# One decoder kernel, mamba stage: the state inputs of two slots are spread back to back, the sums run two slots behind, and the small work has other slots

## What is computed

```
xz = x @ in_w.T;  xi, z = split(xz)                 # 512 features each
u = silu(causal_conv4(xi) + conv_b)
xdbl = u @ xp_w.T                                   # 16 for dt, 16 for B, 16 for C
dt = softplus(xdbl[:, :16] @ dt_w.T + dt_b)
h[t] = exp(dt[t] * A) * h[t-1] + (dt[t] * u[t]) * B[t]     # 512 features x 16 states
y[t] = sum_n(h[t][:, n] * C[t][n]) + u[t] * D
out = (y * silu(z)) @ out_w.T
```

## Time and profile before

| what | value |
|---|---|
| median of three runs | 2918.92 us |
| the profiled execution | 2914.82 us |
| its span | 2913.0 us |
| PE matmul busy, of the span | 94% |
| PE weight load busy | 62% |
| DVE / ACT / POOL busy | 75% / 60% / 53% |
| scans, instructions and mean | 1024, 1203 ns |
| hC, instructions and mean | 512, 2369 ns |
| dA, instructions and mean | 1024, 710 ns |
| spread products, instructions and busy | 8192, 595.9 us |
| sum products, instructions and busy | 4120, 563.5 us |

### The profile page before, as it was taken

How to read it: one execution, slowest core, us unless ns; L and a number is a source line. 1 busy time by engine, 2 the same in 40 slices (tenths; PEclk the granted TensorE clock), 3 DMA queues, 4 the chain that set the end, 5 groups by cost and what they waited for, 6 DMA issues and landing times. The chain is left out here.

```text
span 2913.0 us, 55381 instructions
## 1 busy us (share of the span) xinstructions
PE 2741.4 (94%) x19289; PEld 1815.9 (62%) x19330; DVE 2188.3 (75%) x3270; ACT 1756.4 (60%) x2899; POOL 1550.5 (53%) x850
## 2 busy tenths in 40 slices
PE   5999999999999999999999959999999999999996
PEld 2777777777777777777777634545454545454423
DVE  3988988898889889888988768484847474747463
ACT  5778877877877788678768413444444444444332
POOL 1888889888988888898889721111111111111010
PEclk8999999999999999999999979999999999999978
DMA  3022211212220222112112071505050505050500
GB/s 116 31 76 77 70 53 63 97 33 70 81 83 32 76 77 67 56 62 98 33 66 97 8 161 41 78 18 80 15 88 8 89 6 94 2 94 2 79 2 15
DMA packets 113354, 174.50 MB, mean 60 GB/s; under 512 B 15232, under 2 KB 88064, under 8 KB 113056
## 3 DMA queue, kind: packets, MB, share of 16 engines
q1 hardware_dynamic: 113104, 171.34, 23.0%
HBM read 148.38 MB, written 22.94 MB: 59 GB/s over the span
## 5 line engine op out<-in xcount | busy, mean ns | idle before, releaser
L925 DVE TENSOR_TENSOR_SCAN h<-dA,pair 128x512 f32<-128x512 f32 x1024 | 1177.2, 1203 | 142.1 <-PE pair L448 111.5
L1067 POOL TENSOR_TENSOR hC<-h,C_rep 128x1024 f32<-128x1024 f32 x512 | 1197.9, 2369 | 87.1 <-DVE h L925 83.1
L678 ACT ACTIVATE dA<-delta,cols 128x511 f32<-128x511 f32 x1024 | 664.5, 710 | 98.7 <-DVE h L925 97.7
L448 PEld LDWEIGHTS pair<-diagB,duT 64*128 64x128 f32 x8192 | 498.1, 188 | 239.7 <-issue 194.0
L448 PE MATMUL pair<-diagB,duT 64*128 64x128 f32 x8192 | 595.9, 285 | 20.1 <-issue 10.2
L539 PE MATMUL y_bank<-ident,hC 128*128 128x128 f32 x4120 | 563.5, 280 | 9.4 <-POOL hC L1067 7.8
L539 PEld LDWEIGHTS y_bank<-ident,hC 128*128 128x128 f32 x4120 | 442.0, 141 | 73.9 <-POOL hC L1067 10.4
L1791 DVE CUSTOM_DVE_ANT_0 masked<-pair,mask_bias 128x512 f32<-128x512 f32 x512 | 321.9, 687 | 28.3 <-PE pair L1304 14.5
L1864 POOL TENSOR_SCALAR rstd<-mv 128x4 f32<-128x4 f32 x24 | 11.6, 484 | 563.5 <-DVE mv L1643 563.5
L1536 ACT ACTIVATE pr<-pair 128x1024 f32<-128x1024 f32 x256 | 248.5, 1021 | 94.2 <-PE pair L1304 83.8
L448 PE MATMUL general<-xnT,w_in 128*128 128x512 f32 x512 | 253.0, 605 | 5.9 <-ACT zs L678 3.1
(11 more groups left out here) (173 smaller groups left out, 3156.9 us busy)
## 6 DMA issues: line engine op xcount, KB each, us to landing
C_rep<-c_rows SPq DMA_DIRECT2D x128, 512.0 KB, 3.9
w_in<-w_in SPq DMA_DIRECT2D x16, 1024.0 KB, 4.8
qk_parts<-qk_part SPq DMA_DIRECT2D x48, 256.0 KB, 2.5
k_st<-qk_parts SPq DMA_DIRECT2D x48, 256.0 KB, 9.0
q_st<-qk_parts SPq DMA_DIRECT2D x48, 256.0 KB, 8.8
x_in<-x SPq DMA_DIRECT2D x18, 512.0 KB, 4.3
w_out<-w_out SPq DMA_DIRECT2D x17, 512.0 KB, 4.4
mid<-x_out SPq DMA_DIRECT2D x9, 512.0 KB, 6.4
```

The source lines that it names most:

```text
L448: return pe.matmul(o, lhsT, rhs, start=start, stop=stop)
L678: return act.activation(o, i, fn, **kw)
L925: last = dve.tensor_tensor_scan(h[:, g % 4, i, :], dA[:, g % 4, i, :], dBu[:, i, :], 0.0, ALU.mult, ALU.add)
L1067: pool.tensor_tensor(hC[:, g % RING], h[:, g % 4], C_rep[:, 2 * j:2 * j + 2, :], ALU.mult).then_inc(s_hC.sem, 1)
```

## The change

It spreads slots p + 1 and p + 2 one after the other at every even slot, where it spread p + 1 at every slot; SUM_LAG goes from 3 to 2; nearly all tables change; the load of w_in waits for z as well as for xi; and `apart` may leave a place in the rotation of banks empty so that a yb does not follow an xd in its bank. Arithmetic and number of instructions on PE, DVE, ACT and POOL in a unit stay as they are.

```
--- before.py
+++ after.py
@@ -87,41 +87,54 @@
     return before, loop, [key for key in loop if key[0] not in skip]
 
 
-XI_AT = {1: (1, 1), 2: (5, 5), 3: (15, 16), 0: (25, 25)}
-Z_AT = {3: (13, 14), 0: (26, 26), 1: (29, 29), 2: (30, 31)}
-DT_AT = {1: 1, 2: 4, 3: 17, 0: 24}
-TR_AT = {1: 5, 2: 11, 3: 19, 0: 27}
-OP_AT = ((7, 8), (10, 10))
+XI_AT = {1: (0, 0), 2: (8, 8), 3: (10, 12), 0: (26, 26)}
+Z_AT = {3: (14, 14), 0: (25, 25), 1: (28, 29), 2: (31, 31)}
+DT_AT = {1: 2, 2: 5, 3: 17, 0: 23}
+TR_AT = {1: 5, 2: 12, 3: 21, 0: 29}
+OP_AT = ((4, 7), (8, 8))
 XP_AT = (21, 21, 21, 21)
-BT_AT = 23
-NF_AT = (20, 23)
-SUM_LAG = 3
+BT_AT = 24
+NF_AT = (19, 23)
+SUM_LAG = 2
 RING = 4
-BACK_AT = {3: 4, 0: 13, 1: 19, 2: 30}
-
-XI_OUT = {1: 0, 2: 5, 3: 17, 0: 26}
-Z_OUT = {3: 16, 0: 28, 1: 30, 2: 31}
-SUM_OUT = {3: 0, 0: 9, 1: 18, 2: 27}
-SOFT_AT = {1: 0, 2: 4, 3: 18, 0: 25}
-TR_OUT = {1: 4, 2: 13, 3: 21, 0: 29}
+BACK_AT = {3: 2, 0: 10, 1: 18, 2: 28}
+
+XI_OUT = {1: 0, 2: 9, 3: 14, 0: 27}
+Z_OUT = {3: 16, 0: 27, 1: 30, 2: 31}
+SUM_OUT = {3: 0, 0: 9, 1: 17, 2: 25}
+SOFT_AT = {1: 1, 2: 7, 3: 18, 0: 24}
+TR_OUT = {1: 6, 2: 12, 3: 20, 0: 30}
 SILU_AT = 19
 XD_OUT, BT_OUT = 21, 24
-NF_OUT = (20, 24)
-RES_AT = 11
-DIAG_ACT = {1: 28, 3: 30, 5: 30, 7: 31}
-SKIP_AT = {3: 1, 0: 10, 1: 16, 2: 28}
+NF_OUT = (21, 24)
+RES_AT = 9
+DIAG_ACT = {1: 26, 3: 28, 5: 30, 7: 30}
+SKIP_AT = {3: 0, 0: 8, 1: 17, 2: 25}
 FIRST_AT = (14, 18)
-LN_AT = ((11, 11), (14, 14))
-
-TAP_AT = {1: (3, 3, 4), 2: (8, 9, 10), 3: (17, 17, 18), 0: (27, 27, 28)}
-GATE_AT = {3: 4, 0: 15, 1: 20, 2: 31}
-DELTA_AT = {1: 3, 2: 6, 3: 18, 0: 26}
-ADD_AT = (9, 11)
-STATS_AT = ((0, 0, 0), (13, 13, 13))
-
-DU_AT = {1: 2, 2: 6, 3: 17, 0: 24}
-DIAG_POOL = {0: 23, 2: 28, 4: 31, 6: 31}
-RSTD_AT = (3, 11)
+LN_AT = ((10, 11), (16, 17))
+
+TAP_AT = {1: (2, 4, 4), 2: (10, 10, 10), 3: (15, 16, 17), 0: (28, 28, 29)}
+GATE_AT = {3: 4, 0: 12, 1: 21, 2: 30}
+DELTA_AT = {1: 4, 2: 8, 3: 20, 0: 26}
+ADD_AT = (8, 10)
+STATS_AT = ((0, 0, 0), (12, 14, 15))
+
+DU_AT = {1: 3, 2: 9, 3: 19, 0: 25}
+DIAG_POOL = {0: 26, 2: 29, 4: 31, 6: 31}
+RSTD_AT = (6, 14)
+
+
+def apart(keys, banks=3):
+
+    out = []
+    for key in keys:
+        while key[0] == "yb":
+            held = [old for old in out[len(out) - banks::-banks] if old is not None] if len(out) >= banks else []
+            if not held or held[0][0] != "xd":
+                break
+            out.append(None)
+        out.append(key)
+    return out
 
 
 def mamba_keys():
@@ -154,7 +167,7 @@
             keys += [key for _, key in sorted(at)]
         return keys
 
-    return before, batch(4), batch(2) + [("yb", 2 * KI)] + [("op", TT + jj) for jj in range(TT // 2)]
+    return before, apart(batch(4)), apart(batch(2) + [("yb", 2 * KI)] + [("op", TT + jj) for jj in range(TT // 2)])
 
 
 BEFORE, AFTER = "before", "after"
@@ -171,10 +184,13 @@
             held[k] = key
         final = {}
         for n, key in enumerate(loop):
-            final[n % len(banks)] = key
+            if key is not None:
+                final[n % len(banks)] = key
         for name, keys in (("loop", loop), (AFTER, after)):
             held = {}
             for n, key in enumerate(keys):
+                if key is None:
+                    continue
                 k = n % len(banks)
                 self.where[name, key] = (k, ("this", held[k]) if k in held else ("last", final[k]))
                 held[k] = key
@@ -397,6 +413,8 @@
                     if live(M):
                         sp.wait_ge(*G.full(("xi", KI * d + 2), it))
                         settle(sp)
+                        sp.wait_ge(*G.full(("z", KI * d), it))
+                        settle(sp)
                         load_in(d)
                     if live(N):
                         sp.wait_ge(*G.full(("dt", KI * d + 2), it))
@@ -592,8 +610,9 @@
                 for d in range(2):
                     U, N, M = 2 * b + d, 2 * b + d + 1, 2 * b + d + 2
                     for p in range(UP):
-                        if p + 1 < UP or live(N):
-                            spread_du(U, p + 1)
+                        for g in (p + 1, p + 2):
+                            if p % 2 == 0 and (g < UP or live(N)):
+                                spread_du(U, g)
                         sum_states(U, p - SUM_LAG)
                         for i, k in enumerate((3, 0, 1, 2)):
                             if p == BACK_AT[k]:
```

## The result

The changed kernel takes 2850.84 us (median of 4 runs, 2848.7 to 2855.99) against 2918.21 for the one before, a ratio of 0.9771 with a 95% interval of 0.9754 to 0.9788: 67 us faster. The profiled execution has a span of 2854.1 us; the mamba stage ends at about 1594 us instead of 1657.

The account below looks back on a forecast made before the run. PE was taken as the bound. A unit goes from 100.1 to 95.7 + 0.7 + 1.0 + 0.2 + 0.5 = 98.1 us; 14 units plus 1 at the end gain 29 us, giving 2890 us, range 2870 to 2926.

Parts of the forecast that it names:

- PE is the bound: Mamba stage: PE has 98.6 us of work in a unit of 100.1, so work taken off PE shortens it.
- That rival: DVE is the bound already and nothing comes of the change: 2900 to 2925 us, chance 0.18.
- the change of mode: PE between half-row spreads and full-row work: 0.09 us each, two fewer per two slots, 46 us for 256 pairs.
- the list of a unit: PE's work in one batch and direction of 32 slots: 98.6 us before, 95.7 after.
- Two spreads in a row: PE at even slots: second spread taken at 1.0 us, bounds 0.9 and 1.69; 1.69 everywhere would add 177 us, excluded.
- The idle time: PE per unit after the change: 0.7 us loop head, plus waits of 1.0, 0.2 and 0.5.
- the loop's head: PE idle before the first spread of every second unit, 1.41 us; counted as 0.7 us a unit.
- Its places: PE waits around slots 14 to 18, 1.0 us on average; x_proj 0.2; near misses by POOL and ACT 0.5.
- The dt product of slot 17: PE product taking the bank the slot's last tap frees: 0.3 us too early, inside the wait already counted.
- The sum of slot 15 in direction 0: PE sum needing POOL's hC: following POOL's queue from slot 14, reached with -0.15 us to spare.
- The slower rival: Spread p+2 behind scan p at even slots: the meeting costs more than the modes, 2926 or 2946 us, chance 0.15.
- The last unit: End of the mamba stage, set by DVE: gains about nothing, 1 us from one sum fewer after the last scan.

Follow-up runs that it names:

- e5: Changed kernel with the whole sum p-2 placed between the two spreads of an even slot: 2917.05 us, ratio 0.9983 to the kernel before.
- e10: Changed kernel with each of the twelve convolution taps of a unit on DVE working on 16 columns instead of 509 to 511: 2838.1 us, ratio 0.9726.
- e11: Changed kernel with ACT's second normed block at slot 23 instead of 24 and the first diagonals at 27 instead of 26: 2861.2 us, ratio 0.9799.
- e1: Kernel before with only the two spreads back to back at every even slot, old tables and sums three behind: 3060.05 us, ratio 1.0476.
- e8: Changed kernel with block 3's taps and convolution start one slot earlier, and the second normed block at slot 23: 2852.31 us, ratio 0.9786.
- e2: Changed kernel with one spread per slot again, new tables and lag of two kept: 3015.98 us, ratio 1.0326 to the kernel before.
- e3: Changed kernel with sums three slots behind instead of two (SUM_LAG = 3): 3026.38 us, ratio 1.0382 to the kernel before.
- e4: Changed kernel with the first of the 8 transposes of sum p-2 done between the two spreads: 2909.53 us, ratio 0.9965 to the kernel before.

## Why the prediction was right in kind and wrong in size

- **PE is the bound** (98.6 us of work in a unit of 100.1): right. e5 puts 5.6 us a unit of changes of mode back and 4 of them show. The rule under which DVE came first (the Trainium skill, "Perfetto Trace Analysis", "Identifying the Most-Contended Engine": for TensorE the share of its weight loads, or its FLOP utilization, in place of matmul busy time, and occupancy for the others) would have had the change give about 2919. The measurement decides against it here: PE with its loads busy 76% was the bound, DVE with 88% was not. That rival is dead, and e10 says the same of the changed kernel.
- **The term that was mis-sized is the change of mode**, taken as 0.09 us each and 0.18 per pair of slots, 46 us in all. It is 0.35, 89 us. That step failed: the list of a unit went from 98.6 to 93.0 us and not to 95.7. The error was in reading. I took the distance across the border (last couple to first transpose, 0.20 for 0.11) and did not look at the one after it. And I checked it with two sums of 0.93 and 1.02 us that both stood behind a spread: the 0.06 of the second transpose was in both and cancelled. The 16 products of a spread in 1.09 us against 8 x 0.11 = 0.88 would have shown it; I used that very product for the bound of the second spread.
- **Two spreads in a row**, taken at 1.0 us with bounds 0.9 and 1.69: 0.99. The exclusion of 1.69 was right. That the second spread takes 0.99 where one entered from full-row work takes 1.09 is the same missing 0.10 us, and the sum did not book it: it took 1.0 and left the two slots at 4.06, where 3.88 was measured.
- **The idle time**: 0.7 for the loop's head and 1.7 of waits, 2.4 in all, predicted; 95.8 - 93.0 = 2.8 measured. The total is near, in part by luck. The head is less: the idle time put down to issue before spreads fell from 8.9 to 2.4 us, 0.2 a unit. The waits are more. The rows of loads above give, over 13.9 units, 1.0 us a unit for scans, 0.5 for hC, 0.4 for xnT and 0.35 for the last tap, 2.25 in all; as loads can wait without cost, these shares are rough.
- **Its places** held in part. The dt product of slot 17 waits for the last tap, as said, and duT is close to late (e11). From spread 18 to spread 19 it is 4.52 us in the changed kernel and 3.85 in e10, where the taps are short (means of six units of direction 1). The sum of slot 15 in direction 0, put at -0.15 us, is late for its hC. Not foreseen were z of slot 25 waiting for xnT (0.5 us of idle PE in each unit of direction 0), and that scan 0 too is late at the head of the loop (DVE stands 1.34 us idle before it, put down to issue) and with it spread 2. The head (first two rows) and the sum (third) in one unit of direction 0:

```profile
261.93 1.16 PE L466 MATMUL pair<-diagB,duT 64*128 64x128 f32 x16 [0.30 <-issue]
263.37 1.16 PE L466 MATMUL pair<-diagB,duT 64*128 64x128 f32 x16 [0.28 <-DVE h L944]
...
316.13 1.09 PE L557 MATMUL y_bank<-ident,hC 128*128 128x128 f32 x8 [0.56 <-POOL hC L1086]
```

- **The slower rival** (the meeting costs more than the modes) did not come true with these tables. It is the nearest to what e1 did, but e1 lost 140 us, and its one wait that was tested was two engines crossing within one slot, which totals of a pair do not hold.
- **The last unit** gained nothing, as said: 92.7 us before and 93.4 after.

The account closes: 15 units x 4.2 us (99.6 to 95.4 on average from the first scan of the stage to that of the last unit) is 63 us; the other 4 of the 67 are within the spread of the runs (2849 to 2856 for the changed kernel).

What stays open is what the rest of PE's idle 2.8 us would give back: about 0.2 are the loop's head and 0.6 come from the taps. For the other 2.0 the rows name scans, hC and xnT, but no run separates them, and e8 and e11 show that a wait taken out here can come back elsewhere.

## What to carry to other kernels

Read the price of a border between two kinds of work from the distance of starts over the whole run of each kind, entered and not entered from the other kind, not from the one interval at the border. When a wait is moved ahead of an engine's small work, look up in every other engine's list who uses that work in the same slot: e1 and e2 came out 140 and 96 us slower than the kernel before and e3 176 us slower than the changed kernel, where the whole change gained 67. And a version whose parts are each 3% slower alone can be 2% faster together, so test such parts by putting one cost back into the whole (e4, e5), not only by adding them one at a time.

## What the runs showed of the hardware that was not expected

A change between spreads (two products of 64 rows side by side) and products or transposes of 128 rows costs at two places: 0.09 us before the first product of the new kind, and another 0.10 us (into spreads) or 0.06 us (into transposes) before the second. A pair of changes, into spreads and back, is 0.35 us, seen as 4.23 to 3.88 us for two slots and as 3.79 to 4.14 us when one transpose was put between two spreads (e4). The late second product is not a matter of the change alone. In the changed kernel, spread 2 at 263.37 stands directly behind spread 1 and waits only for its scan, and the sum at 316.13 stands behind another sum; their second couple and second transpose are late as well (narrow windows as above):

```profile
263.58 0.40 PE L466 MATMUL pair<-diagB,duT 64*128 64x128 f32 x4
```

```profile
316.30 0.38 PE L557 MATMUL y_bank<-ident,hC 128*128 128x128 f32 x2
```

That is 0.21 us for 0.11 and 0.17 for 0.11 with no change of mode, so by these rows a product that starts after a pause is followed late in the same way, and a short wait of PE costs 0.1 us or 0.06 us more than its own length. The number of rows alone does not bring the cost: w_dt products of 81 rows go over into w_in products of 128 at the usual distance (876.11 to 876.97, 0.86 us for two). The Trainium skill, "TensorEngine Tiling (Array Packing)", "Key Properties", says that changing the tiling mode drains TensorE. The trace agrees as far as a delay at the first place goes (0.20 us for 0.11 at the border), though it does not show its cause; that the second product is late too is seen here in the rows alone.
